# Attention stages of a fused two-layer kernel: batch 1's split moved up and shared with ScalarE, and the order of a batch rewritten on three engines

## The reference, cut to what matters

```python
def _L0_attn_ref(x, Wq, bq, Wk, bk, Wv, bv, Wo, bo):   # B, L, D = 8, 256, 128; 16 heads of 8
    q = (x @ Wq.T + bq).reshape(B, L, H, hd)
    k = (x @ Wk.T + bk).reshape(B, L, H, hd)
    v = (x @ Wv.T + bv).reshape(B, L, H, hd)
    q = _apply_rope(q, cos, sin)
    k = _apply_rope(k, cos, sin)
    scores = jnp.einsum('bqhd,bkhd->bhqk', q, k) / np.sqrt(hd).astype(np.float32)
    attn = jax.nn.softmax(scores, axis=-1)
    out = jnp.einsum('bhqk,bkhd->bqhd', attn, v).reshape(B, L, D)
    return out @ Wo.T + bo
def _L1_attn_ref(x, Wq, bq, Wl, bl, Wk, bk, Wv, bv, Wo, bo):
    q = (x @ Wq + bq).reshape(B, S, H, Dh)
    latent = x @ Wl + bl
    k = (latent @ Wk + bk).reshape(B, S, H, Dh)
    v = (latent @ Wv + bv).reshape(B, S, H, Dh)
    ...
x = _layernorm(x + _L0_attn_ref(x, ...), axis=-1)
x = _layernorm(x + _L0_ffn_ref(x, ...), axis=-1)
x = _layernorm(x + _L1_attn_ref(x, ...), axis=-1)
x = _layernorm(x + _L1_ffn_ref(x, ...), axis=-1)
```

## Time and profile before

| what | us |
|---|---|
| runs shown, median (lowest to highest) | 590.81 (587.14 to 593.11) |
| the profiled execution, its own time | 588.97 |
| its span, first to last instruction | 587.0 |
| busy in the span: TensorE / VectorE / ScalarE / GpSimd | 522.6 / 420.2 / 399.7 / 344.9 |
| granted TensorE clock, mean | 0.94 |

### The profile page before, as it was taken

How to read it: one execution, slowest core, us unless ns; L and a number is a source line. 1 busy time by engine, 2 the same in 40 slices (tenths; PEclk the granted TensorE clock), 3 DMA queues, 4 the chain that set the end, 5 groups by cost and what they waited for, 6 DMA issues and landing times.

```text
span 587.0 us, 16199 instructions
## 1 busy us (share of the span) xinstructions
PE 522.6 (89%) x5038; PEld 371.4 (63%) x5038; DVE 420.2 (72%) x1568; ACT 399.7 (68%) x1076; POOL 344.9 (59%) x471
## 2 busy tenths in 40 slices
PE   9899999999779984779999999889999999999950
PEld 7434443457558973534544345658999999999940
DVE  4969989955865304877989995877887788642276
ACT  2178888892524752438888888327788888999824
POOL 4978888261006783684555517455667777777730
PEclk9979999998999996978999999789999999999975
DMA  7465941103001237015565630221222122211463
GB/s 220 68 178 133 255 98 38 39 1 77 3 1 44 47 38 235 3 37 144 146 146 144 162 58 9 65 40 48 53 58 58 57 63 59 60 59 56 130 190 118
DMA packets 82770, 50.43 MB, mean 86 GB/s; under 512 B 44560, under 2 KB 72992, under 8 KB 82560
## 3 DMA queue, kind: packets, MB, share of 16 engines
q1 hardware_dynamic: 75136, 37.32, 24.3%
q0 software_dynamic: 7264, 11.62, 7.7%
q10 hardware_dynamic: 288, 0.46, 0.2%
HBM read 30.17 MB, written 11.87 MB: 72 GB/s over the span
## 4 chain that ended last, share of the span: by engine, by line
PE 66%; DVE 10%; DMA 7%; issue 6%; ACT 6%; POOL 5%; DVEq 0%; SPq 0%; POOLq 0%; ACTq 0%
PE bank L1346 12%; PE bank L1356 11%; PE bank L953 10%; PE bank L936 7%; PE bank L1061 4%; PE bank L918 3%; PE bank L970 3%; ACT prob L1494 3%; DVE W L1973 2%; PE bank L996 2%; DMA parts<-augs,idx_s 2%; PE bank L1162 2%; DMA sum<-rt,idx_s 1%; PE bank L980 1%; PE bank L1328 1%
## 5 line engine op out<-in xcount | busy, mean ns | idle before, releaser
L1804 DVE TENSOR_REDUCE mx<-bank 128x2 f32<-128x512 f32 x256 | 160.7, 685 | 22.6 <-PE bank L918 21.9
L1494 ACT ACTIVATE prob<-bank 128x512 f32<-128x512 f32 x256 | 140.5, 609 | 21.5 <-PE bank L936 19.7
L1678 ACT ACTIVATE queries<-bank,prob 128x128 f32<-128x128 f32 x316 | 90.4, 369 | 19.6 <-PE bank L1346 16.4
L1346 PE MATMUL bank<-keys,prob 128*128 x632 | 85.8, 279 | 0.7 <-issue 0.7
L1356 PE MATMUL bank<-W,queries 128*128 x632 | 84.4, 277 | 0.1
L918 PE MATMUL bank<-keys 32*128 32x256 f16 x512 | 76.1, 279 | 6.1 <-DMA keys<-augs 4.8
L825 POOL DMA_INDIRECT prob<-xs,idx_g x64 | 61.9, 968 | 32.9 <-DVE idx_g L2184 11.3
L936 PE MATMUL bank<-QT,keys 32*128 32x256 f16 x512 | 74.1, 278 | 5.7 <-ACT prob L1494 3.0
L1346 PEld LDWEIGHTS bank<-keys,prob 128*128 128x128 f32 x632 | 76.8, 192 | 3.5 <-issue 1.9
L1356 PEld LDWEIGHTS bank<-W,queries 128*128 128x128 f32 x632 | 76.7, 192 | 2.2 <-issue 1.1
L953 PE MATMUL bank<-prob,augs 128*32 128x256 f32 x1024 | 77.6, 392 | 0.2
(11 more groups left out here) (292 smaller groups left out, 971.0 us busy)
## 6 DMA issues: line engine op xcount, KB each, us to landing
W<-in_w SPq DMA_DIRECT2D x48, 256.0 KB, 3.8
sum<-zero SPq DMA_DIRECT2D x3, 1024.0 KB, 8.9
xs<-X SPq DMA_DIRECT2D x2, 768.0 KB, 5.2
prob<-xs,idx_g POOLq DMA_INDIRECT x80, 2.6
XB<-sum SPq DMA_DIRECT2D x1, 1024.0 KB, 4.9
Y<-sum SPq DMA_DIRECT2D x4, 256.0 KB, 4.6
W<-sum SPq DMA_DIRECT2D x4, 256.0 KB, 5.0
parts<-augs,idx_s POOLq DMA_INDIRECT x64, 2.3
```

The costliest lines, as they stand in the source:

```text
L1346: last = nc.tensor.matmul(bank[2 + p % 2][:, P * f:P * f + P], wc[:, p % 4, P * f:P * f + P], xsT2[:, bass.ds(at, 1), :], start=True, stop ...
L1494: nc.scalar.activation(prob[:, v % 8, :, :], st_bank(b, v)[:, :], ACT.Exp, scale=SCALE).then_inc(exp_done, 1)
L1678: last = nc.scalar.activation(hid2[:, p % 4, f, :], bank[2 + p % 2][:, P * f:P * f + P], ACT.Gelu, bias=wc[:, p % 4, WB + f:WB + f + 1])
L1804: nc.vector.tensor_reduce(m_at, bank[S1B[(16 * i + u) % 3]][:, :].rearrange("p (j k) -> p j k", j=2), AX.X, ALU.max).then_inc(s1_used, 1)
```

## The change

Four things.

1. `build_aug` skips the four high copies when b is 1. A new ScalarE function, `split_high`, makes them, keys first: in layer 0 after iteration 0, in layer 1 at the head of iteration 0.
2. In layer 1, projection (1, 1) is issued in one piece before batch 0's transposes, and ScalarE copies both halves of batch 1's projection before it copies the turned keys of batch 0.
3. `max_transposes` waits for the projection copies first, then, in iteration 1, issues 14 small matmuls on constants (`warm`, into bank 2), then waits for `m_ready`.
4. The order of an iteration is new. On TensorE, `st` units follow a pair of `s1` units of the two other row groups, in fours where that goes; both halves of value product 3 follow `st` 0 and 1, both halves of product 0 stand together, `out_transposes` come at u = 9 and `out_product` between `st` 10 and 11 at u = 13. On ScalarE the copies of the projection stand after exponentials 2, 3 and 4, 5; `out_evac` after 6, 7; the bank copy (pair 0) after 8, 9. On VectorE the residual is added after reduction 13 and no longer after 15.

```diff
--- before.py
+++ after.py
@@ -50,12 +50,6 @@
 WROW = W2AT + F
 FIRST, LAST = -6, 4
 LOW, NROUND, COARSE = 9, 10, 7
-
-
-def soft_units(u):
-
-    return {2: [0], 3: [2], 4: [3], 6: [4, 5], 7: [6], 8: [7], 9: [8], 10: [9], 11: [10], 12: [11],
-            14: [12, 13]}.get(u, [])
 
 
 def turn_step(t):
@@ -541,6 +535,8 @@
                     engine.tensor_tensor(s4[:, t, 0:H, :], s4[:, t, 0:H, :], bias, ALU.add).then_inc(q_biased, 1)
             for t in range(2):
 
+                if b == 1:
+                    continue
                 if lay == 1:
                     engine.wait_ge(q_biased, 2 * b + t + 1)
                 qin = s4[:, t, 0:H, :].unsqueeze(2).to_broadcast([P, H, 2, HD])
@@ -972,9 +968,11 @@
 
             def max_transposes(lay, i, nxt):
 
-                pe.wait_ge(m_ready, i + NB * lay)
                 if i < NB - 1:
                     pe.wait_ge(qkv_ready, 2 * (i + NB * lay) + 4)
+                if i == 1:
+                    warm(14, 2)
+                pe.wait_ge(m_ready, i + NB * lay)
                 for j in range(NJ):
                     for t in range(2):
                         last = nc.tensor.transpose(half[M5][:, L * j + P * t:L * j + P * t + P],
@@ -1010,43 +1008,58 @@
                     s1(lay, i, par, u)
                     if lay == 0 and i == 0:
                         warm(4, 2)
-                    if u == 1 and tail_on:
-                        bt(lay, i - 2, 0)
-                    if u == 1 and soft_on:
-                        max_transposes(lay, i, nxt)
-                    if u == 1 and tail_on:
-                        av(lay, i - 2, par, 2, 1)
-                        av(lay, i - 2, par, 3, 0)
-                    if u == 3 and soft_on:
-                        st(lay, i - 1, nxt, 1)
-                    if joined and u == 1:
-                        front_query(1, 1)
-                    if joined and u == 3:
-                        front_latent_product(1, 1)
-                    if lay == 1 and i < 2 and u == 5:
-                        join_turn(2 + i)
+                    if u == 1:
+                        if tail_on:
+                            bt(lay, i - 2, 0)
+                        if soft_on:
+                            max_transposes(lay, i, nxt)
+                        if tail_on:
+                            av(lay, i - 2, par, 2, 1)
+                    if u == 3:
+                        if soft_on:
+                            st(lay, i - 1, nxt, 0)
+                            st(lay, i - 1, nxt, 1)
+                        if tail_on:
+                            av(lay, i - 2, par, 3, 0)
                     if u == 3 + late and proj_on and lay == 1:
                         front_latent(lay, i + 2, par)
                     if u == 3 and tail_on:
                         av(lay, i - 2, par, 3, 1)
+                    if u == 4 and soft_on:
+                        st(lay, i - 1, nxt, 2)
+                        st(lay, i - 1, nxt, 3)
+                    if u == 5 and lay == 1 and i < 2:
+                        join_turn(2 + i)
                     if u == 5 + late and proj_on:
                         front_proj(lay, i + 2, par, 0)
-                    if u == 5 and tail_on:
+                    if u == 7 and soft_on:
+                        st(lay, i - 1, nxt, 4)
+                        st(lay, i - 1, nxt, 5)
+                    if u == 7 and tail_on:
                         bt(lay, i - 2, 1)
-                    if u in (7, 9) and soft_on:
-                        av(lay, i - 1, nxt, 0, u // 9)
                     if u == 7 + late and proj_on:
                         front_proj(lay, i + 2, par, 1)
-                    if u in (10, 12) and soft_on:
-                        av(lay, i - 1, nxt, 1, u // 12)
+                    if u == 9 and soft_on:
+                        st(lay, i - 1, nxt, 6)
+                        st(lay, i - 1, nxt, 7)
+                        av(lay, i - 1, nxt, 0, 0)
+                        av(lay, i - 1, nxt, 0, 1)
+                    if u == 9 and tail_on:
+                        out_transposes(lay, i - 2)
+                    if u == 11 and soft_on:
+                        st(lay, i - 1, nxt, 8)
+                        st(lay, i - 1, nxt, 9)
+                        av(lay, i - 1, nxt, 1, 0)
+                    if u == 13 and soft_on:
+                        av(lay, i - 1, nxt, 1, 1)
+                        st(lay, i - 1, nxt, 10)
                     if u == 13 and tail_on:
-                        out_transposes(lay, i - 2)
-                    if u == 15 and tail_on:
                         out_product(lay, i - 2)
-                    if soft_on:
-                        for v in soft_units(u):
-                            st(lay, i - 1, nxt, v)
+                    if u == 13 and soft_on:
+                        st(lay, i - 1, nxt, 11)
                     if u == 15 and soft_on:
+                        st(lay, i - 1, nxt, 12)
+                        st(lay, i - 1, nxt, 13)
                         av(lay, i - 1, nxt, 2, 0)
 
             def hold(lay, n):
@@ -1430,6 +1443,7 @@
                         front_latent_product(0, t)
                     front_latent(lay, 1, 1)
                     front_proj(lay, 1, 1, 0)
+                    front_proj(lay, 1, 1, 1)
                     query_transposes(lay, 0, 0)
                     key_transposes(lay, 0, 0)
                     join_turn(1)
@@ -1518,7 +1532,7 @@
                 if tail_on:
                     exps(lay, i - 2, (14, 15))
                 if joined:
-                    front_evac(lay, 1, 1, 1)
+                    split_high(lay, 1)
                     join_evac(2)
                 if soft_on:
                     max_queries(lay, i)
@@ -1534,16 +1548,17 @@
                 if proj_on:
                     front_evac(lay, i + 2, par, 0)
                 if soft_on:
-                    exps(lay, i - 1, range(4, 9))
+                    exps(lay, i - 1, (4, 5))
                 if proj_on:
                     front_evac(lay, i + 2, par, 1)
                 if soft_on:
-                    exps(lay, i - 1, (9, 10, 11))
+                    exps(lay, i - 1, (6, 7))
                 if tail_on:
                     out_evac(lay, i - 2)
                 if soft_on:
+                    exps(lay, i - 1, (8, 9))
                     ot_evac(lay, i - 1, 0)
-                    exps(lay, i - 1, (12, 13))
+                    exps(lay, i - 1, range(10, 14))
 
             def act_last(lay):
 
@@ -1566,6 +1581,26 @@
                 if not (isinstance(b, int) and g == 0):
                     act.wait_ge(bt_done, 2 * g + pair - 1)
                 nc.scalar.copy(OT[:, pair, :, :], bank[OTB][:, :]).then_inc(ot_ready, 1)
+
+            def split_high(lay, b):
+
+                g = b + NB * lay
+                act.wait_ge(aug_ready, 2 * g)
+                act.wait_ge(tq2_done, 2 * (g - 1)) if lay == 1 else act.wait_ge(rope_step, 9 * g + 9)
+                A = aug[b % 2]
+                s4 = v4(qk_of(lay, b % 2) if lay == 1 else rt1)
+                for t in range(2):
+                    kin = s4[:, t, H:2 * H, :].unsqueeze(2).to_broadcast([P, H, 2, HD])
+                    kout = A[:, t, H:2 * H, 0:4 * HD].rearrange("p h (r y) -> p h r y", r=2)[:, :, :, 0:HD]
+                    if lay == 1:
+                        act.wait_ge(qkv_ready, 2 * g + t + 1)
+                    nc.scalar.copy(kout, kin).then_inc(split_step, 1)
+                for t in range(2):
+                    qin = s4[:, t, 0:H, :].unsqueeze(2).to_broadcast([P, H, 2, HD])
+                    qout = A[:, t, 0:H, 0:2 * HD].rearrange("p h (r x) -> p h r x", x=HD)
+                    if lay == 1:
+                        act.wait_ge(q_biased, 2 * b + t + 1)
+                    nc.scalar.copy(qout, qin).then_inc(split_step, 1)
 
             def lat_evac(b):
                 act.wait_ge(lat_done, b + 1)
@@ -1734,12 +1769,15 @@
                     front_evac(lay, 0, 0, 1)
                     lat_evac(1)
                     join_normalise(1)
+                    front_evac(lay, 1, 1, 0)
+                    front_evac(lay, 1, 1, 1)
                     keys_evac(lay, 0, 0, 0)
                     keys_evac(lay, 0, 0, 1)
-                    front_evac(lay, 1, 1, 0)
                     join_evac(1)
                 for i in range(NB):
                     act_iteration(lay, i, i % 2, i > 0, i < NB - 1, i > 1)
+                    if lay == 0 and i == 0:
+                        split_high(lay, 1)
                 act_last(lay)
                 if lay == 1:
                     sums_cleared()
@@ -1807,7 +1845,7 @@
                         norm(lay, i - 2, 0)
                     if u == 7 and tail_on:
                         norm(lay, i - 2, 1)
-                    if u == 15 and tail_on:
+                    if u == 13 and tail_on:
                         output_added(lay, i - 2)
 
                 dve.wait_ge(s1_used, 16 * g + 16)
```

## The result

The changed kernel takes **597.44 us** (median of 4 runs, 596.85 to 599.45), the kernel before 590.2 beside it (median of 4, 587.14 to 593.11): 7.2 us more, a ratio of 1.0114 with a 95% interval of 1.0071 to 1.0157. The profiled execution took 597.02 us, its span 595.2, 8.2 over the span before.

A forecast was written before the change was run, and what follows sets the result against it. Bound: the hand-over between TensorE and ScalarE through two PSUM banks. Starts -0.85 - 1.3, batch 1 -2.0 - 1.8, order +3.5 and +6.0, correction -1.2: +2.4 on 588.97 gives 591.4, as median 593.2; range 587 to 600.

The forecast's parts named there:

- the start of layer 1: Layer 1, first iteration and batch 1: M moves from 259.95 to 258.6, -1.3 us; batch 1 at 13.5, -1.8.
- The order: From batch 2: periods near 13.8 us (layer 0), 14.6 (layer 1), 13.2 without projections; +3.5 and +6.0 us by layer.
- the bank copy's wait: ScalarE's copy before exponential 2 could start only 2.75 us after M, ending at 3.22; before, ready when ScalarE came.
- TensorE's wait of 0.4 before unit 5: In the new order unit 5 waits on TensorE until 4.35 us after M; 0.4 counted as lost.
- The start of layer 0: M of batch 1 moves from 26.92 to about 26.1, -0.85 us; batch 1 at 13.0, -2.0.
- the copy's price: Batch 1's split: four copies moved to ScalarE take 1.2 us in all, upper bound 2.0 to 2.4.
- M: Start of the eight transposes of the query maxima, opening each batch; batch 1's forecast at about 26.1 and 258.6 us.
- the fourteen warm matmuls: Before batch 1's maxima transposes: 0.8 us, free in a wait that VectorE ends; uncovered, 0.8 in each layer.
- C: Clock still falls behind M in batch 1 of both layers; 2.0 + 1.8 us lost, median 597.0; chance 0.21.
- A: TensorE's own time bounds batches and groups of four save it; full batches fall to 12.5, 575 to 579; chance 0.07.
- B: The order is neutral, stalls merely moved; only the earlier batch 1 counts, -6 us, median 585; chance 0.15.
- D: ScalarE makes batch 1's split late, so M stays at 26.9 and 259.9; +8.4 us, median 599.2; chance 0.04.

The follow-up runs named there:

- run 9: Changed kernel without layer 1's latent product and its copy for batches 4 to 7 (stale latents used): 596.58 us, ratio 1.0078.
- run 4: Changed kernel with score units 10 and 11 together ahead of the output product: 664.97 us, ratio 1.0123, on a chip where the kernel before takes 658.67.
- run 3: Changed kernel with the second back transposes ahead of unit 5's group: 671.79 us, ratio 1.0179, on a chip where the kernel before takes 658.67.
- run 5: Changed kernel again, nothing altered: 598.49 us, ratio 1.015 to the kernel before.
- run 6: Changed kernel with four warm matmuls behind each score unit of layer 1's first iteration too: 603.01 us, ratio 1.0184.
- run 10: Changed kernel with warm matmuls in TensorE's holes ahead of layer 1's first iteration: 599.47 us, ratio 1.012.
- run 1: Changed kernel with the old order, only batch 1's start changed: 661.15 us, ratio 1.0023, on a chip where the kernel before takes 658.67.
- run 7: Kernel before with batch 1's split on ScalarE in layer 0 only, old order and old start of layer 1: 588.99 us, ratio 0.9984.
- run 8: Kernel of run 1 once more (start alone, old order), a single execution: 590.75 us, beside a median of 590.27.
- run 11: Run 7's kernel plus 54 warm matmuls before layer 1's batch 1, eight behind score units 2 and 3 of batch 1 in both layers: 590.41 us, ratio 0.9971.
- run 12: Same kernel as run 11, measured once more: 588.48 us, ratio 0.9967.
- the candidate: The kernel of run 11 and run 12, run 7's kernel with added warm matmuls: 590.41 and 588.48 us, ratios 0.9971 and 0.9967.

## Why the prediction was right, and where it was wrong

The time, 597.44, lies in the range and 4.2 us above the forecast of 593.2; it is slower by 1.1%, on the edge of what the prediction counted as the same. The change itself was 7.2 us where 2.4 had been forecast, so that the range held owes much to its width of 13 us. In the profiled execution the sum is 5.8 too low: 4.7 in the start of layer 1, 2.1 in batches 2 to 5 of layer 0, and -0.9 in stretches that the change doesn't touch (+0.73 between the layers, -1.66 at the end).

**The order: right, its mechanism in the main.** Forecast periods 13.8, 14.6 and 13.2; measured 13.74, 14.52, and 13.24 and 13.14. Of the reasons these are shown. Exponential 2 waits for the bank copy (3.22 forecast, 3.23 measured); in layer 1 for the latent copy too (3.99, 4.00), and taking the latents out removes just that 0.77 (run 9). The output product between units 10 and 11 costs 0.28 of every period, which came back with one unit moved (run 4). That leaves nothing of the loss in layer 0, but 0.50 in a batch without projections; the prediction lays this to the bank copy's wait, and no run tests it. The order costs 3.6 us in layer 1's four even batches, 1.1 in layer 0's and 3.1 in the four without projections. What the hand work read wrongly is which stall matters: it counted TensorE's wait of 0.4 before unit 5 as lost, and filling it made the batch of layer 0 0.16 longer (run 3; 0.07 shorter in layer 1). There the wait was free, because ScalarE had its next unit.

**The start of layer 0: right** in the copy's price (four in 1.3 us, forecast 1.2 from a 128x256 copy), in M (26.07, forecast 26.1) and in batch 1 at nearly the full clock (13.12, forecast 13.0). Its remark that GpSimd would hinder VectorE no longer is borne out too, by the small steps above (0.18 and 0.30 us where they took 0.41 and 0.65). The transposes landed near 24.9 instead of 24.3, still without harm. Behind M it is not a dependable gain: over the seven profiles with this start and the new order or a variant of it (runs 3, 4, 5, 6, 9 and 10 and the first), batches 1 and 2 together take 28.0 us in the first, 28.3, 28.0, 28.3, 28.6 and 29.2 in runs 5, 6, 9, 10 and 3, and 26.6 in run 4 with its shorter order, where the full clock gives 27.0 (13.12 and 13.88; 26.6 in run 4). In six of seven the clock fell in the one or the other, in run 3 in both. The kernel before has 28.4 there, with the clock down for 6.8 us; this start with the old order has 29.1, 27.4, 26.5, 26.8 and 28.3 (runs 1, 7, 8, 11 and 12).

**The start of layer 1: wrong.** The step was "M moves from 259.95 to 258.6, -1.3", with batch 1 at "13.5: -1.8". What it says of GpSimd is right (split over 5.5 us after the query transposes, 5.4 by the forecast). Its silent assumption, that nothing but that split decides M there, failed: in all nine profiles with projection (1,1) ahead the clock fell in the middle of the first iteration (4.6 to 6.1 us behind the query transposes, 5.3 in the first), and M came 15.6 to 16.3 us behind them instead of 14.51, 23.6 in run 6. Of the five profiles without it three have the fall at 11.8 to 12.8 us and M at 14.51, but the two of the candidate fall at 5.8 and 5.9 as well; so that moving the projection brings the fall forward is likely, not shown. To this come 0.64 us of the fourteen warm matmuls, priced at nothing: at half clock they end after the maxima. With that, terms of -3.1 became +1.6, and this is most of the miss; a second part is the clock's fall in even batches of layer 0, +2.4 in the profiled execution, which no rival foresaw.

**The rivals.** C has the right size (597.0 as a median) for partly the wrong place: it put both falls behind M of batch 1, and in layer 1 the fall came before M. Its "if" for layer 0 comes true in some executions. A fell as a forecast: no period of batches 2 to 5 is below 13.46. But its premise was miscounted. In the traces a full batch has nine groups of 32-row matmuls in the old order as well as in the new, not ten and nine, in both layers; so this change saves no such group, and what one group fewer is worth remains untested here. B fell by the periods. D's time is close as well (597.4 for the profiled execution, 597.02 measured), but its mechanism is absent: no DMA wait decided M in either layer.

**Open.** What exactly brings the clock down in layer 1's first iteration. Shown is only that filling the holes between TensorE's records behind the query transposes doesn't prevent it (run 6), nor does making those ahead of them smaller (run 10); each was profiled once. Also open are what else the order costs where there are no projections, and what one group of 32-row matmuls fewer is worth.

## What to carry to other kernels

Where two engines hand work to and fro through two banks, price an order by when the next unit's input is ready for the engine that is fed, not by how little the other waits (in run 3 filling such a wait made the batch of layer 0 0.16 us longer), and look with suspicion at a long product queued between two units of such a chain (0.64 us of it cost 0.28 a batch here). A small step that used to fill a wait (here the latent copy) can be paid in full when the new order removes that wait (0.77 us a batch here, where the old order's two layers differ by 0.16), so work out every variant of the loop body by hand. A start that is gained where the clock is seen to fall is no gain until the clock is shown to hold there, in more than one execution (in layer 1 start and batch 1 together took 29.86 us in run 8, 29.81 in the kernel before).

## What the runs showed of the hardware that had not been expected

TensorE's clock fell while its records lay end to end and then stayed low. In run 1 they lie so from 14.20 us on, and the clock fell at 17.3; in run 6 from 250.92, and it fell at 254. For 14 us in run 1 and 18.6 in run 6 it was at 0.50 with TensorE busy all the time, on score units of 32 rows and 128-column warm matmuls, in run 6 on transposes, latent products and projections too. The falls of the kernel before, at 28.6 and 257.3 us, stand beside the idle stretches of the earlier trace rows, the first 2.0 us behind the end of its stretch, the second 0.9 us into its own. So a full row of busy time did not protect the clock in runs 1 and 6, and the warm matmuls that failed to hold it cost more there: a turn of one score unit and four of them took 1.07 us in run 1 at 0.50, and 0.65 at 1.00 in the same run's first turns.

VectorE's small steps on 32 columns took 0.41 and 0.65 us while GpSimd was at work (kernel before) and 0.18 and 0.30 while it idled (changed kernel), in the same place of the kernel.

In the same program the fall can move by a batch from one execution to the next (batches 1 and 2 of layer 0 took 13.12 and 14.90 us in the changed kernel's first profile, 14.38 and 13.88 in run 5), while the periods of batches 3 to 5 at the full clock repeat to 0.01 us (13.74, and 13.73 to 13.75 in run 5); a comparison of profiles should therefore be made from the latter, and one of whole times from many runs.
